# The half steps of both layers of an interaction network as split fp32r steps, and one full split step of layer 1 made whole

## What is computed

```python
# x0: (B=2048, 39, 16); W0: (39*39, 128); W1: (39*64, 128)
z0 = einsum('bid,bjd->bdij', x0, x0).reshape(B, 16, 39*39)
cur0 = relu(einsum('bdk,kl->bld', z0, W0))
next_h, direct0 = split(cur0, 2, axis=1)           # 64 rows each
z1 = einsum('bid,bjd->bdij', x0, next_h).reshape(B, 16, 39*64)
cur1 = relu(einsum('bdk,kl->bld', z1, W1))
h = concatenate([direct0, cur1], axis=1).sum(-1)   # (B, 192)
h = concatenate([h, dense_ctx], axis=1)
y = relu(relu(h @ W_top1 + b_top1) @ W_top2 + b_top2) @ W_top3
```

## Time and profile before

| | |
|---|---|
| three runs | 1534.05, 1535.93, 1537.34 us; median 1535.93 |
| profiled execution | 1532.73 us; span 1530.9 us |
| PE, DVE, ACT, POOL busy | 1448.7, 1374.5, 841.2, 993.5 us |
| granted clock of TensorE | full but for parts of the first 120 us |

### The profile page before, as it was taken

How to read it: one execution, slowest core, us unless ns; L and a number is a source line. 1 busy time by engine, 2 the same in 40 slices (tenths; PEclk the granted TensorE clock), 3 DMA queues, 4 the chain that set the end, 5 groups by cost and what they waited for, 6 DMA issues and landing times.

```text
span 1530.9 us, 15059 instructions
## 1 busy us (share of the span) xinstructions
PE 1448.7 (95%) x4496; PEld 790.7 (52%) x4496; DVE 1374.5 (90%) x1277; ACT 841.2 (55%) x865; POOL 993.5 (65%) x628
## 2 busy tenths in 40 slices
PE   0289999999999999999999999999999999999999
PEld 0144455555555555555555555555555555555565
DVE  0168899999999999999999999999999999999981
ACT  0156555556566555566565555566566555565554
POOL 6788888888888867878587877878587870000000
PEclk9989999999999999999999999999999999999999
DMA  3498978888989888888888888889888887887600
GB/s 88 99 228 214 230 188 214 208 208 206 222 206 213 203 210 211 207 209 204 218 205 217 205 209 208 205 206 211 219 205 205 210 215 203 203 203 195 172 0 1
DMA packets 124578, 294.06 MB, mean 192 GB/s; under 512 B 38016, under 2 KB 48144, under 8 KB 124368
## 3 DMA queue, kind: packets, MB, share of 16 engines
q1 hardware_dynamic: 98000, 264.62, 69.9%
q10 hardware_dynamic: 6528, 23.33, 4.6%
q0 software_dynamic: 19968, 5.15, 3.2%
HBM read 269.61 MB, written 23.34 MB: 191 GB/s over the span
## 4 chain that ended last, share of the span: by engine, by line
PE 83%; POOL 9%; issue 3%; DVE 3%; DMA 1%; ACT 0%; DVEq 0%; ACTq 0%
PE psB L372 39%; PE psA L372 12%; POOL emb L352 9%; PE psB L390 6%; PE psB L397 6%; PE psB L393 6%; PE psA L380 2%; PE psB L380 2%; PE psA L393 2%; PE psA L390 2%; PE psA L397 2%; PE psA L364 2%; DVE z_lo L664 1%; DVE z L656 1%; DVE z_split L656 1%
## 5 line engine op out<-in xcount | busy, mean ns | idle before, releaser
L352 POOL DMA_INDIRECT emb<-in_tbl,ids_all x624 | 993.3, 1592 | 264.3 <-issue 187.1
L372 PE MATMUL psB<-z,w 128*128 128x512 f32 x1536 | 690.5, 596 | 3.6 <-DVE z L656 3.6
L553 ACT ACTIVATE z_hi<-z_split 128x1024 fp32r<-128x1024 f32 x288 | 305.0, 1059 | 486.5 <-DVE z_split L656 441.9
L372 PEld LDWEIGHTS psB<-z,w 128*128 128x128 f32 x1536 | 289.2, 190 | 367.6 <-issue 329.1
L656 DVE TENSOR_TENSOR z<-h_quad,x_lay 128x1024 f32<-128x1024 f32 x352 | 417.5, 1216 | 15.5 <-PE psB L372 8.7
L664 DVE TENSOR_TENSOR z_lo<-z_split,z_hi 128x1024 fp32r<-128x1024 f32 x288 | 351.6, 1221 | 2.3 <-ACT z_hi L553 2.3
L656 DVE TENSOR_TENSOR z_split<-h_quad,x_lay 128x1024 f32<-128x1024 f32 x224 | 270.9, 1221 | 1.3 <-DMA x_lay<-x_rows 1.3
L533 ACT ACTIVATE h_quad<-psA 32x1024 f32<-32x1024 f32 x256 | 259.5, 1014 | 3.8
L372 PE MATMUL psA<-z,w 128*128 128x512 f32 x512 | 244.1, 600 | 9.5 <-DVE z L656 9.5
L390 PE MATMUL psB<-z_hi,w_hi 128*128 128x512 f32 x448 | 158.3, 434 | 0.0
L372 PEld LDWEIGHTS psA<-z,w 128*128 128x128 f32 x512 | 97.7, 192 | 109.3 <-issue 103.4
(11 more groups left out here) (61 smaller groups left out, 847.2 us busy)
## 6 DMA issues: line engine op xcount, KB each, us to landing
x_lay<-x_rows SPq DMA_DIRECT2D x1152, 128.0 KB, 5.9
x_more<-x_rows SPq DMA_DIRECT2D x64, 512.0 KB, 6.7
bases<-x_rows SPq DMA_DIRECT2D x64, 468.0 KB
x_rows<-x_ring ACTq DMA_DIRECT2D x32, 512.0 KB
x_lay<-x_rows SPq DMA_DIRECT2D x64, 256.0 KB, 4.0
emb<-in_tbl,ids_all POOLq DMA_INDIRECT x624
x_last<-x_rows SPq DMA_DIRECT2D x64, 128.0 KB, 6.9
x_rows<-x_ring ACTq DMA_DIRECT2D x32, 200.0 KB
```

What stands on the lines that cost most here:

```text
L352: nc.gpsimd.indirect_dma_start(emb[t % 2][:, f * D:(f + 1) * D], None, tables[f], bass.IndirectOffsetOnAxis(ids_all[:, t, f:f + 1], 0)).th ...
L372: mm = nc.tensor.matmul(ps[:, cs], w, z[WHOLE_NO[place] % NZ][0:k, cs], start=first, stop=last)
L553: nc.scalar.activation(z_hi[n % NS][0:k, :], z_split[n % NS][0:k, :], ACT.Copy).then_inc(z_hi_made, 1)
```

## The change

The half steps become split: step 6 is added to SPLIT0, step 1 to SPLIT1. Of the full steps of layer 1, 3, 4, 8, 9, 10, 13, 14 were split; now 2, 3, 8, 9, 13, 14 are, so there is one less, 4 and 10 are whole, and 2 is split. `half_product` runs three pairs of matmuls on z_hi and z_lo; `high`, `make` and `low` take their columns from `shape_of`.

```diff
-SPLIT0 = (1, 4)
-SPLIT1 = (3, 4, 8, 9, 10, 13, 14)
+SPLIT0 = (1, 4, 6)
+SPLIT1 = (1, 2, 3, 8, 9, 13, 14)
...
+HALF_AT = {at0(u, STEPS0 - 1) for u in range(UNITS)} | {at1(u, 1) for u in range(UNITS)}
+def shape_of(place):
+
+    half = place in HALF_AT
+    return P, BANK if half else C
...
-            def half_product(ps, place, w, last):
-
-                pe.wait_ge(z_made, place + 1)
-                for n in range(2):
-                    rows = slice(n * HROWS, (n + 1) * HROWS)
-                    mm = nc.tensor.matmul(ps[:, n * BANK:(n + 1) * BANK], w[rows, :],
-                                          z[WHOLE_NO[place] % NZ][rows, 0:BANK], start=False, stop=last)
+            def half_product(ps, place, w_hi, w_lo, last):
+
+                n = SPLIT_NO[place]
+                pe.wait_ge(z_hi_made, n + 1)
+                for w, part in ((w_hi, z_hi), (w_lo, z_hi), (w_hi, z_lo)):
+                    if part is z_lo:
+                        pe.wait_ge(z_lo_made, n + 1)
+                    for c in range(2):
+                        rows = slice(c * HROWS, (c + 1) * HROWS)
+                        mm = nc.tensor.matmul(ps[:, c * BANK:(c + 1) * BANK], w[rows, :], part[n % NS][rows, 0:BANK],
+                                              start=False, stop=last and part is z_lo)
                 mm.then_inc(z_used, 1)
...
-            def high(place, k):
-
+            def high(place):
+
+                k, cols = shape_of(place)
                 n = SPLIT_NO[place]
                 act.wait_ge(z_made, place + 1)
                 if n >= NS:
                     act.wait_ge(z_used, SPLIT_AT[n - NS] + 1)
-                nc.scalar.activation(z_hi[n % NS][0:k, :], z_split[n % NS][0:k, :], ACT.Copy).then_inc(z_hi_made, 1)
+                nc.scalar.activation(z_hi[n % NS][0:k, 0:cols], z_split[n % NS][0:k, 0:cols], ACT.Copy).then_inc(z_hi_made, 1)
...
+            def low(place):
+
+                k, cols = shape_of(place)
                 n = SPLIT_NO[place]
                 dve.wait_ge(z_hi_made, n + 1)
...
             for s in range(STEPS0):
                 step0(0, s)
                 low_before(at0(0, s))
+            low(at0(0, STEPS0 - 1))
```

More of the change, by code:

```diff
@@ L403, in step0 @@
                 if s == STEPS0 - 1:
-                    half_product(half(psA, u), at0(u, s), w0[:, ORDER0.index(s), :], True)
+                    n = SPLIT0.index(s)
+                    half_product(half(psA, u), at0(u, s), w0_hi[:, n, :], w0_lo[:, n, :], True)
                 elif s in SPLIT0:
@@ L414, in step1 @@
                 if s == 1:
-                    half_product(half(psB, u), at1(u, s), w1[:, WHOLE1.index(s), :], False)
+                    n = SPLIT1.index(s)
+                    half_product(half(psB, u), at1(u, s), w1_hi[:, n, :], w1_lo[:, n, :], False)
                 elif s in SPLIT1:
@@ L563, in body @@
                     if s in SPLIT1:
-                        high(at1(u, s), P)
+                        high(at1(u, s))
                     if s in AFTER and AFTER.index(s) in SPLIT0 and u + 1 < UNITS:
-                        high(at0(u + 1, AFTER.index(s)), P)
+                        high(at0(u + 1, AFTER.index(s)))
                     if s == 7 and u >= 1:
@@ L579, in _ @@
             spread_x(1)
-            high(at0(0, SPLIT0[0]), P)
+            high(at0(0, SPLIT0[0]))
             keep_x(1)
-            high(at0(0, SPLIT0[1]), P)
+            high(at0(0, SPLIT0[1]))
+            high(at0(0, SPLIT0[2]))
             relu0(0)
@@ L644, in _, with make @@
         def _(dve):
-            def make(place, cols, a, b):
+            def make(place, a, b):
+                k, cols = shape_of(place)
                 if place in SPLIT_NO:
@@ L655, in make @@
                     out = z[n % NZ]
-                nc.vector.tensor_tensor(out[:, 0:cols], a[:, 0:cols], b[:, 0:cols], ALU.mult).then_inc(z_made, 1)
-            def low(place, k):
+                nc.vector.tensor_tensor(out[0:k, 0:cols], a[0:k, 0:cols], b[0:k, 0:cols], ALU.mult).then_inc(z_made, 1)
+            def low(place):
+                k, cols = shape_of(place)
                 n = SPLIT_NO[place]
@@ L663, in low @@
                     dve.wait_ge(z_used, SPLIT_AT[n - NS] + 1)
-                nc.vector.tensor_tensor(z_lo[n % NS][0:k, :], z_split[n % NS][0:k, :], z_hi[n % NS][0:k, :].bitcast(FP),
+                nc.vector.tensor_tensor(z_lo[n % NS][0:k, 0:cols], z_split[n % NS][0:k, 0:cols], z_hi[n % NS][0:k, 0:cols].bitcast(FP),
                                         ALU.subtract).then_inc(z_lo_made, 1)
@@ L670, in step0 @@
                     dve.wait_ge(half_b_loaded, 32 * len(HALF_B) * (u + 1))
-                    make(at0(u, s), BANK, half_a, half_b)
+                    make(at0(u, s), half_a, half_b)
                     return
@@ L679, in step0 @@
                     dve.wait_ge(more_loaded[t - 1], 16 * u + 16)
-                make(at0(u, s), C, base[c], more[t])
+                make(at0(u, s), base[c], more[t])
             def step1(u, s):
@@ L685, in step1 @@
                     dve.wait_ge(h_half_made, u + 1)
-                    make(at1(u, s), BANK, h_half, x_last)
+                    make(at1(u, s), h_half, x_last)
                     return
@@ L695, in step1 @@
                     dve.wait_ge(h_quad_made[k], u + 1)
-                make(at1(u, s), C, h_quad[u % 2][k] if s else h_pair, lay(u, m))
+                make(at1(u, s), h_quad[u % 2][k] if s else h_pair, lay(u, m))
             def low_before(place):
-                if place - 1 in SPLIT_NO:
-                    low(place - 1, P)
+                if place - 1 in SPLIT_NO and place - 1 != at0(0, STEPS0 - 1):
+                    low(place - 1)
             def sum_over_d(r, n):
```

## The result

The changed kernel takes 1586.2 us (median of 5 runs, 1584.0 to 1589.5) against 1535.93 (5 runs, 1534.1 to 1540.2): ratio 1.033, 95% interval 1.031 to 1.034. It is 50 us slower. The forecast was 1590, range 1579 to 1604. The profiled execution took 1584.7 us, its span is 1582.9.

A forecast was written before the change was run, and what follows sets the result against it. PE bounded the kernel, DVE close behind; new waits decide: 27 bodies x 1.86 = +50.1, gather-paced body +2.6, last two +1.4, total +54.1. 1532.7 becomes 1586.9, on the median's scale 1590 us, range 1579 to 1604.

The forecast's parts named there:

- Turn against S: In each body, the 8 transposes on PE start at S + 6.53 us, after ACT's z_hi and DVE's row.
- S: End of ACT's spread_x in a body, put at 13.86 us after the end of layer 0's half step.
- The half step in fp32r: Each half step on PE takes 1.18 us against 1.26 in fp32; 0.87 if nothing is lost between pairs.
- From the turn to E: From the 8 transposes to the end of layer 0's half step (E): 24.71 us after, 24.08 before.
- The body: One repeated body of the kernel grows from 43.24 to 45.10 us, +1.86; 27 bodies give +50.1 us.
- The gather-paced body: In the early body whose spread_x end a gather sets whatever PE does, the end moves from 218.95 to 221.6, +2.6 us.
- The two last bodies: The last two bodies have no spread_x, so each costs +0.7 us, 1.4 together.
- Other waits: Between the turn and the end of layer 0's half step, split steps 8 and 9 add no further PE waits.
- (a): Rival: PE's sum alone decides, as ACT or DVE run further ahead; +6 us, 1542; chance 0.06.
- (b): Rival: half steps lose nothing between pairs (0.87 each) and S doesn't bind; 13 us faster, 1523; chance 0.05.
- (c): Rival: row halves don't run side by side in fp32r, half step 2.17 us; 1617; chance 0.05.
- (d): More waits at hand-overs or a third PE wait: up to +0.3 us a body, 1600; inside the forecast's 0.84.

The follow-up runs named there:

- experiments 1: Changed kernel with ACT's wrap and spread_x moved behind the z_hi of layer 1's steps 1 and 2: ratio 1.012 to the kernel before, +19.1 us.
- experiment 2: Changed kernel with wrap, spread_x and relu0's last copy, r, moved behind the same z_hi of layer 1's steps 1 and 2: ratio 1.004 to the kernel before, +7.1 us.

## Why the prediction was right, step by step

The mechanism was right: the z_hi behind spread_x, DVE standing for it, PE waiting twice. The time was nearly right partly by luck. On the two profiled executions the forecast was +54.1 and the measured difference of the spans is 52.0. The 27 bodies gave 6.2 us less than forecast, the start 3.8 more and the end 0.4 more.

- **What bounds**: right. The body of 43.24 us was the unit in which the change was paid.
- **Turn against S**: I had S + 6.53, it is S + 6.41. ACT takes the z_hi up 0.1 us before spread_x's recorded end, not 0.03 after; all else stands as worked out. S itself is 13.84, as forecast (13.86). The two waits of PE, forecast at 0.4 to 0.9, are 0.36 and 0.77 in the body shown.
- **The half step in fp32r**: I had 1.18 with its edges; from 762.72 to 763.63 it takes 0.91, with the edges about 1.1. The loss of 0.10 is there between the first two pairs (0.34) and not between the second and third (0.24). The third pair takes 0.33 up to the next step. So my term was too large by 0.06 to 0.09, and the value for nothing lost (0.87) too small. From the turn to E: 24.62, I had 24.71.
- **The body**: 44.86 against 45.10; over 27 bodies 43.9 us instead of 50.1. This is the main error of the sum, 6 us.
- **The gather-paced body**: I had +2.6. Against the first trace it was +6.4, of which 3.9 is a gather that landed later; between the mean of the three traces of before and that of the two of after it is 4.8. "Whatever PE does" holds in so far as the body does wait for a gather (4.84 us in that trace), but the gather's place moves by 3 us between executions of one kernel, and the sum took it as fixed. This error ran the other way.
- **The two last bodies**: I had +1.4 for both. The body with E(30) to E(31) went from 42.77 to 43.63, +0.9, and the end behind it by +0.9 in the first pair of traces.
- **Other waits**: none was forecast at steps 8 to 14, none is there. One reading was wrong without harm: I let DVE reach the blocked z_lo at E + 13 to 14, and it does so at E + 11.2 to 12.6, ahead of S in either case.
- **The rivals**: (a) and (b) fell with experiments 1 and 2, and experiment 2 shows what (a) would have looked like once S is taken away: +0.08 a body. (c) fell: the halves of the rows do run side by side in fp32r. (d) was not needed.
- **The scale**: the profiled execution lay 3.2 us under the median of before; after, the one profiled lies 1.5 under its own. The forecast of 1590 less the 6 us of the bodies and plus the 2 to 4 of the start gives 1586 to 1588, against 1586.2.

The rule of the Trainium skill's page "TensorEngine Tiling (Array Packing)", section Tiling Modes (Key Properties), that a change of tiling mode drains the TensorE, was weighed against the rows of before. The rows after stand between the two readings: 0.09 lost at entry and about 0.10 at exit, as much again between the first two pairs (0.34 from start to start), and almost nothing between the second and third (0.24).

## What to carry to other kernels

When a step is moved to a form that needs a second engine, look where that engine stands in its own program at that moment: here 12.6 us of copies and one more of 1.1 stood ahead of a 0.6 us operation. DVE, whose program is in a fixed order, passed that wait on to all that stood behind. Engine totals don't show it: DVE's busy time even fell (1374.5 to 1369.2 us), and PE's own work a body stayed the same to 0.08 us. Adding up each engine's row from one common event does show it: it gave the turn to 0.15 us and the body to 0.24 us here. If the step must be moved, move behind it the copies that are only wanted later: that alone gave back 1.54 of 1.62 us a body. Even then look for what is gained: with DVE as full as it is here, no variant beat the kernel before.

## What the runs showed of the hardware

- Two fp32r matmuls on the two halves of the rows, 64x512, run side by side: three pairs took 0.91 us (762.72 to 763.63), about 0.30 a pair, where a pair over the full 128 rows, one after the other, takes 0.46. In fp32 two such pairs took 1.06.
- DVE operations of 128x1024 fp32 with everything at hand started every 1.137 us (778.47 to 781.88 is three of them), and the next operation 0.60 behind one of 128x512. The row of five behind S took the same time in all 27 bodies (turn 6.40 to 6.42 behind S).
- ACT began a copy 0.1 us before the recorded end of the copy before it, behind r and behind spread_x alike (776.19 against 775.27 + 1.02 = 776.29, and 777.22 against 777.31).
